# Layer 0's norm: logarithms and exponentials in three batches, centre and squares on VectorE, scaling shared with GpSimd, the last bias part sent from two queues

## What is computed

```python
def _layernorm(x, gamma, beta, eps=1e-05):
    mu = jnp.mean(x, axis=-1, keepdims=True)
    var = jnp.var(x, axis=-1, keepdims=True)
    return (x - mu) * jax.lax.rsqrt(var + eps) * gamma + beta
...
x = _layernorm(pair, gamma, beta)
q = (x @ Wq).reshape(B, L, L, N_HEAD, D_HID) * SCALING
...
bias = x @ Wb
gate = jax.nn.sigmoid(x @ Wg + bg)
attn = jnp.einsum('bijhd,bikhd->bijkh', q, k)
attn = attn + bias[:, None]
attn = jax.nn.softmax(attn, axis=-2)
out = jnp.einsum('bijkh,bikhd->bijhd', attn, v).reshape(B, L, L, N_HEAD * D_HID)
out = gate * out
return out @ Wo + bo
```

## Time and profile before

| | |
|---|---|
| median of 3 runs | 1290.49 us (1289.76 to 1291.64) |
| the profiled execution, device time | 1290.73 us |
| its span, first to last instruction | 1288.9 us |
| PE, PEld, DVE, ACT, POOL busy | 86%, 60%, 56%, 44%, 25% of the span |
| `layer0_norm`'s first matmul | 58.96 us |
| last bias DMA issued | at 155.2 us |
| first L703 of attention | 163.27 us |

### The profile page before, as it was taken

The page is one execution under the profiler, slowest core; times in us unless marked ns, Lnnn a source line. Parts: engine busy times, 40 slices in busy tenths (PEclk is TensorE's granted clock), DMA queues, the critical chain, the costliest instruction groups (busy, mean ns, idle before and its releaser), DMA issues. The chain is left out here.

```text
span 1288.9 us, 25804 instructions
## 1 busy us (share of the span) xinstructions
PE 1104.4 (86%) x9639; PEld 771.7 (60%) x9639; DVE 715.9 (56%) x3496; ACT 569.2 (44%) x1161; POOL 324.7 (25%) x466
## 2 busy tenths in 40 slices
PE   3666288888888886998599999999999999999778
PEld 2422076666666663344477677767776777777577
DVE  2511066666666665222566766676666766676235
ACT  1299466666555553001244444444444444444200
POOL 0100055555555552100012221222122211222211
PEclk9697589999999997998699999999999999999969
DMA  7000000000000000000000000000000000000002
GB/s 151 1 1 4 5 3 2 2 2 2 3 2 2 2 3 1 1 1 9 1 2 1 1 2 2 1 1 2 1 1 2 1 2 1 1 1 1 1 28 108
DMA packets 11488, 11.38 MB, mean 9 GB/s; under 512 B 4324, under 2 KB 9188, under 8 KB 11364
## 3 DMA queue, kind: packets, MB, share of 16 engines
q1 hardware_dynamic: 9266, 9.08, 2.6%
q10 hardware_dynamic: 2098, 0.65, 0.3%
HBM read 5.14 MB, written 4.23 MB: 7 GB/s over the span
## 5 line engine op out<-in xcount | busy, mean ns | idle before, releaser
L1451 PE MATMUL quad<-theta,nat 128*128 128x512 f32 x512 | 240.7, 593 | 0.0
L639 POOL TENSOR_TENSOR nat<-nat,arena 128x512 f32<-128x512 f32 x128 | 132.6, 1048 | 114.6 <-DVE arena L703 114.6
L1258 POOL TENSOR_TENSOR nat<-nat,const 128x512 f32<-128x512 f32 x32 | 40.6, 1268 | 444.0 <-DVE nat L1389 444.0
L1283 ACT ACTIVATE flat<-quad 128x256 f32<-128x256 f32 x256 | 94.9, 384 | 87.5 <-PE quad L1459 72.7
L1459 PEld LDWEIGHTS quad<-flat 128*128 128x128 f32 x768 | 104.6, 190 | 46.5 <-ACT flat L1283 25.1
L1459 PE MATMUL quad<-flat 128*128 128x128 f32 x768 | 123.8, 284 | 2.8 <-ACT flat L1283 1.7
L1451 PEld LDWEIGHTS quad<-theta,nat 128*128 128x128 f32 x512 | 87.5, 191 | 61.7 <-issue 61.7
L703 DVE CUSTOM_DVE_ANT_0 nat<-quad,arena 128x128 f32<-128x128 f32 x512 | 113.2, 282 | 9.8 <-PE quad L788 9.8
L662 ACT ACTIVATE nat<-bank 128x512 f32<-128x512 f32 x128 | 69.6, 595 | 101.7 <-PE bank L796 101.7
L1360 DVE SCALAR_TENSOR_TENSOR flat<-nat,c,duo 128x128 f32<-128x128 f32 x64 | 22.0, 344 | 106.5 <-PE duo L1470 106.5
L667 ACT ACTIVATE nat<-nat 128x512 f32<-128x512 f32 x128 | 77.2, 633 | 5.6 <-POOL nat L639 5.5
(11 more groups left out here) (382 smaller groups left out, 2285.1 us busy)
## 6 DMA issues: line engine op xcount, KB each, us to landing
out<-nat SPq DMA_DIRECT2D x16, 256.0 KB, 2.0
arena<-flat SPq DMA_DIRECT2D x64, 4.0 KB
const<-in_constants ACTq DMA_DIRECT2D x1, 400.5 KB, 3.2
arena<-in_L_conv_Ws SPq DMA_DIRECT2D x1, 240.0 KB
flat<-arena SPq DMA_DIRECT2D x3, 32.0 KB, 4.3
nat<-in_x SPq DMA_DIRECT2D x4, 0.2 KB, 11.9
arena<-in_L_conv_Wq ACTq DMA_DIRECT2D x1, 32.0 KB, 6.1
arena<-in_L_conv_Wk ACTq DMA_DIRECT2D x1, 32.0 KB, 6.7
```

The source lines that it names most:

```text
L639: pool.tensor_tensor(scored, scored, of_head(least[b], h).broadcast_to([128, ROWS, L]), ALU.subtract).then_inc(lowered, 1)
L1258: pool.tensor_tensor(quarters(rem), quarters(rem), ident.unsqueeze(1).broadcast_to([128, ROWS, 128]), ALU.add).then_inc(diag_added, 1)
L1283: act.activation(zs[half][k % 2], m.quad[:, HALF * half:HALF * (half + 1), place * C:(place + 2) * C], ACT.Copy).then_inc(z_ready[half], 1)
L1451: return pe.matmul(m.quad[:, n, :], vT[:, col(n)], m.theta[:, part, :], start=(part == 0), stop=False, skip_group_check=True)
```

## The change

- In `layer0_norm` DVE now reads each PSUM centre once: it adds the shift and writes it to `z` (`keep_centre`, `centre_kept`), and squares it from there into one of four buffers. ACT does neither squares nor bias rows.
- ACT takes logarithms of banks 0 to 7, then their exponentials, then 8 to 11, then 12 to 15. `rstd` of all 16 banks stays in `nat`.
- GpSimd scales banks 0 to 7 (after L463's work), DVE banks 8 to 15 after all its centres; DVE keeps the bias rows.
- PE's variance matmul runs two banks behind the centre. Bias matmuls of chunk 0 come after the variance of bank 9, of chunk 1 after bank 11, of chunks 2 and 3 after bank 15. The shift matmul comes first.
- SP sends chunks 0 to 2 in the block. The 16 DMAs of chunk 3 move into `layer0_attention`'s block: eight on SP at once, eight on ACT after q and k of group 0 are kept.
- `wo` is loaded with the other weights on ACT's queue (ahead of theta_w and alpha_raw) and halved in `load_and_prepare`; `pick` is set there too.

```diff
@@ load_and_prepare
+        (m.wo[:, :], args["L0_conv_Wo"]),
         (theta_raw, args["L2_conv_theta_w"]),
...
+            step(pool.memset(m.pick[:, :, :], 0.0))
+            for h in range(HEADS):
+                step(pool.memset(m.pick[:, h, h:h + 1], 1.0))
...
             dve.tensor_copy(m.c0[:, :], coef[:, 0:1])
+            dve.tensor_scalar(m.wo[:, :], m.wo[:, :], 0.5, None, ALU.mult)
@@ layer0_norm
-    squares = [m.take(CH) for _ in range(2)]
-    logs, rstd = ([m.nat[:, (4 * n + b) * CH:(4 * n + b + 1) * CH] for b in range(4)] for n in range(2))
+    squares = [m.take(CH) for _ in range(4)]
-    LAG = 3
+    LAG = 2
+    BATCH_ENDS = (8, 12, 16)
+    POOL_SCALES = BATCH_ENDS[0]
+    BIAS_AFTER = {LAG + 9: (0,), LAG + 11: (1,), LAG + 15: (2, 3)}
@@ gpsimd
+            for q in range(POOL_SCALES):
+                pool.wait_ge(rstd_ready, q + 1)
+                pool.wait_ge(squared, q + 1)
+                pool.tensor_tensor(m.z[:, cols(q)], m.z[:, cols(q)], rstd(q), ALU.mult).then_inc(z_ready, 1)
@@ scalar
-                    act.activation(squares[q % 2], m.bank[q % 4][:, :], ACT.Square, bias=centre_shift).then_inc(squared, 1)
...
+            done = 0
+            for p in range(BANKS):
+                act.wait_ge(var_made, p + 1)
+                act.activation(rstd(p), m.quad[:, p % 2, :], ACT.Ln, bias=m.eps[:, :]).then_inc(logged, 1)
+                if p + 1 in BATCH_ENDS:
                     act.wait_ge(logged, p + 1)
+                    for n in range(done, p + 1):
+                        act.activation(rstd(n), rstd(n), ACT.Exp, scale=-0.5).then_inc(rstd_ready, 1)
+                    done = p + 1
@@ tensor
+            pe.matmul(m.quad[:, 3, 0:1], away, m.shift2[:, :], start=True, stop=True).then_inc(shift_made, 1)
             pe.wait_ge(m.sem("l1_loaded"), 16 * LOADS1)
...
                     if q >= 4:
-                        pe.wait_ge(z_ready, q - 3)
+                        pe.wait_ge(centre_kept, q - 3)
...
-                if 1 <= q <= BANKS:
-                    p = q - 1
+                if q >= LAG:
+                    p = q - LAG
                     pe.wait_ge(squared, p + 1)
                     if p >= 2:
                         pe.wait_ge(logged, p - 1)
...
-                if q == 1:
+                if q == 4:
                     pe.wait_ge(S("early_spread"), 1)
...
-                    pe.wait_ge(z_ready, 4 * chunk + 4)
+                    if 4 * chunk < POOL_SCALES:
+                        pe.wait_ge(z_ready, 4 * chunk + 4)
+                    else:
+                        pe.wait_ge(late_z_ready, 4 * chunk + 4 - POOL_SCALES)
@@ vector
+            def keep_centre(q):
+                dve.wait_ge(centred, q + 1)
+                dve.tensor_scalar(m.z[:, cols(q)], m.bank[q % 4][:, :], centre_shift, None, ALU.add).then_inc(centre_kept, 1)
+                dve.wait_ge(centre_kept, q + 1)
+                if q >= 4:
+                    dve.wait_ge(var_made, q - 3)
+                dve.tensor_tensor(squares[q % 4], m.z[:, cols(q)], m.z[:, cols(q)], ALU.mult).then_inc(squared, 1)
...
+            def scale(first, end):
...
+                    dve.tensor_tensor(m.z[:, cols(q)], m.z[:, cols(q)], rstd(q), ALU.mult).then_inc(late_z_ready, 1)
...
+                    dve.tensor_scalar(m.bias_rows[:, cols(2 * chunk + r)], m.quad[:, 2 + r, :], m.head_bias[:, :], None,
+                                      ALU.add).then_inc(bias_kept, 1)
...
+            for q in range(10, 14):
+                keep_centre(q)
+            keep_bias(0)
+            keep_centre(14)
+            keep_centre(15)
+            keep_bias(1)
+            scale(POOL_SCALES, 12)
+            keep_bias(2)
+            scale(12, 16)
+            keep_bias(3)
@@ sync
-            for chunk in range(CHUNKS):
+            for chunk in range(CHUNKS - 1):
                 sp.wait_ge(bias_kept, 2 * (chunk + 1))
                 for side in range(2):
...
+                    lay_bias(sp, m, chunk, side)
@@ layer0_attention
-            sp.dma_start(wo, args["L0_conv_Wo"]).then_inc(wo_ready, 16)
+            sp.wait_ge(m.sem("z_bias_kept"), 2 * LAST_CHUNK + 2)
+            lay_bias(sp, m, LAST_CHUNK, 0)
...
             keep_qk(0)
+            act.wait_ge(m.sem("z_bias_kept"), 2 * LAST_CHUNK + 2)
+            lay_bias(act, m, LAST_CHUNK, 1)
...
-            pe.wait_ge(pick_ready, 1)
             project_qk(0)
-            pe.wait_ge(S("wo_halved"), 1)
```

More of the change, by code:

```diff
@@ L511, in _ @@
                         pe.wait_ge(logged, p - 1)
-                    pe.matmul(m.quad[:, p % 2, :], same, squares[p % 2], start=True, stop=True).then_inc(var_made, 1)
-                if q == 1:
+                    pe.matmul(m.quad[:, p % 2, :], same, squares[p % 4], start=True, stop=True).then_inc(var_made, 1)
+                if q == 4:
                     pe.wait_ge(S("early_spread"), 1)
@@ L532, in _, with keep_bias @@
         def _(dve):
+            step = m.chain(dve, "dve")
+            def keep_centre(q):
[6 more added lines that the diff above has]
+            def scale(first, end):
+                for q in range(first, end):
+                    dve.wait_ge(rstd_ready, q + 1)
+                    dve.wait_ge(centre_kept, q + 1)
+                    dve.wait_ge(squared, q + 1)
+                    dve.tensor_tensor(m.z[:, cols(q)], m.z[:, cols(q)], rstd(q), ALU.mult).then_inc(late_z_ready, 1)
+            def keep_bias(chunk):
+                for r in range(2):
+                    dve.wait_ge(bias_made, 2 * chunk + r + 1)
+                    dve.tensor_scalar(m.bias_rows[:, cols(2 * chunk + r)], m.quad[:, 2 + r, :], m.head_bias[:, :], None,
+                                      ALU.add).then_inc(bias_kept, 1)
             dve.tensor_scalar(spread, away, m.scale2[:, :], None, ALU.mult).then_inc(spread_ready, 1)
@@ L536, in _ @@
             dve.wait_ge(shift_ready, 1)
-            step = m.chain(dve, "dve")
+            keep_centre(0)
+            keep_centre(1)
             dve.wait_ge(S("early_turned"), 1)
@@ L542, in _ @@
                               m.turned1[0:C, 256:256 + TAPS].unsqueeze(2).broadcast_to([C, TAPS, C]), ALU.mult).then_inc(S("early_spread"), 1)
+            for q in range(2, 6):
+                keep_centre(q)
             dve.wait_ge(S("early_taps"), 1)
@@ L546, in _, with lay_bias, layer0_attention @@
             dve.tensor_copy(m.taps1[:, 512:TAPS * C], m.quad[0:C + 1, 3, 0:C]).then_inc(S("early_kept"), 1)
[L547 to L550 removed]
+            for q in range(6, 10):
+                keep_centre(q)
+            for q in range(10, 14):
+                keep_centre(q)
+            keep_bias(0)
[6 more added lines that the diff above has]
+            keep_bias(3)
         @block.sync
         def _(sp):
[L554 removed]
+            for chunk in range(CHUNKS - 1):
                 sp.wait_ge(bias_kept, 2 * (chunk + 1))
                 for side in range(2):
[L557 to L565 removed]
+                    lay_bias(sp, m, chunk, side)
+def lay_bias(queue, m, chunk, side):
+    for e in range(2):
+        for h in range(HEADS):
+            row = side * C + 32 * e + h
+            first = 2 * (16 * chunk + 8 * side) + e
+            queue.dma_start(m.bias[first:first + 15:2, h * L:(h + 1) * L],
+                            m.bias_rows[row:row + 1, 2 * chunk * CH:2 * (chunk + 1) * CH]).then_inc(m.sem("bias_laid"), 16)
+def layer0_attention(nc, m):
     ident = m.k("ident", 128)
@@ L580, in layer0_attention @@
     factor, gated = m.take(CH), m.take(CH)
[L581 removed]
+    wo, pick = m.wo, m.pick
     least = [m.take(HEADS * ROWS) for _ in range(2)]
[L583 removed]
     sums = m.take(128)
@@ L628, in _ @@
             step = m.chain(pool, "pool")
-            step(pool.memset(pick, 0.0))
-            for h in range(HEADS):
-                step(pool.memset(pick[:, h, h:h + 1], 1.0))
-            pool.sem_inc(pick_ready, 1)
             for g in range(STEPS0):
```

54 lines of the change are left out of this document (11 added, 43 removed).

## The result

| | before | changed |
|---|---|---|
| median | 1290.12 us (1289.27 to 1291.64, 4 runs) | 1270.15 us (1269.03 to 1271.42, 4 runs) |
| ratio, 95% interval | | 0.9843 (0.983 to 0.9855) |
| span of the profiled run | 1288.9 | 1268.0 (device time 1269.75) |
| DVE's first subtraction | 163.27 | 138.89 |
| from there to the end | 1125.6 | 1129.1 |

The kernel is 20.0 us faster, against 22.4 forecast; 1268.0 was predicted and 1270.15 measured, inside the range. The last two lines of the table show two misses with opposite signs: the first subtraction comes 2.0 us earlier than forecast, and 3.5 us are lost again somewhere behind it.

A forecast was written before the change was run, and what follows sets the result against it. ACT's table loads, logarithms and exponentials (4.5 us a bank), then SP's DMA issues at the block's end, bound it. Summed steps moved DVE's first subtraction from 163.27 to 140.9 (-22.4 us), giving 1268.0 us; range 1262.5 to 1276.

The forecast's parts named there:

- Step 1: Start of layer0_norm: with the shift matmul first, the first centre matmul can start at 60.50 instead of 60.85.
- step 8: Loading wo ahead of two other weights on ACT's queue moves the whole first block later: +0.6 us.
- Steps 2 and 3: Norm: TensorE reaches bank 7's variance at 79.95; after the first logarithms and exponential, GpSimd starts at 82.8.
- Step 4: GpSimd's scalings in the norm: 1.27 us each, four done at 87.9.
- Step 6: Norm: DVE's squares wait while GpSimd's scalings read SBUF; +0.9 us, first bias rows kept at 96.4.
- Step 7: Norm: TensorE's granted clock falls around its idle gap before chunk 0's bias matmuls; +1.2 us, bounds 0 or 2.7.
- Step 9: SP's 48 bias DMA issues at 0.66 us take 31.7, ending at 129.9, without waits between chunks.
- Step 10: Entering attention: block's end 0.7, ACT's eight issues 5.2 after q and k, landing 1.7; first subtraction at 140.9.
- So I add nothing: Groups behind the first subtraction: unchanged instructions, TensorE entering at the lower clock in both kernels, so no term added.
- quicker: Rival in the norm: no fall of the clock and no DVE wait for GpSimd; 1265.9 us, chance 0.20.
- shut DVE out through all eight: Rival in the norm: GpSimd's eight scalings block DVE's square until 93.0; 1269.7 us, chance 0.12.
- low all through the stage: Rival: TensorE's clock stays at the lower level throughout the norm; 1286 us, chance 0.03.

The follow-up runs named there:

- the filler: Changed kernel plus five result-less 512-column matmuls on TensorE ahead of chunk 0's bias matmuls in the norm: 1267.61 us, ratio 0.9823.
- the filler, which gives back 3.9: Changed kernel plus four 512-column matmuls on TensorE at layer 2's start, into a bank nothing reads: 1265.88 us, ratio 0.9815.
- batch of one: Changed kernel with each bank's logarithm followed by its exponential (32 table loads), GpSimd still scaling banks 0 to 7: 1277.0 us, ratio 0.9884.
- one-queue kernel: Changed kernel with all 64 bias DMAs sent by SP alone inside the norm's block: 1277.05 us, ratio 0.9883.
- kernels with half the DMAs: Changed kernel with 32 two-row bias DMAs instead of 64: 1254.12 us; with all scalings on VectorE too: 1252.14 us.

## Why the prediction came out right, and where it was off

- **What bounds the kernel**: right. The stage's end moved with the chain named: first batch, four scalings, chunk 0's bias rows, SP's issues, ACT's issues, landing.
- **Step 1 and step 8, start and load of wo**: 60.50 + 0.6 was forecast for the first centre, and it starts at 60.18. The load shows no effect: DVE's instruction behind ACT starts at 19.12 and 19.46 in the two profiles of before, and between 18.89 and 19.85 in the eleven profiles with the load ahead of it; the first centre matmul starts at 60.85 and 61.00 in the one, at 59.25 to 60.52 in the other. Step 8 was mis-sized: 0 instead of 0.6.
- **Steps 2 and 3, to the first scaling**: 83.4 with step 8's 0.6, measured 82.28. 0.9 of the 1.1 comes from the start.
- **Step 4, the scalings**: 1.29 each against 1.27; with the hand-over to TensorE 5.5 us against 5.1.
- **Step 6, the lock**: DVE's square took 1.23 beside GpSimd, against 0.69 alone, so it exists, as sized (0.5 to 0.9). But DVE then idled 8.39 us for the next centre, so on the path it cost 0 instead of 0.9: TensorE's own wait for the scalings and the lower clock behind it covered the lock. With the clock kept high by the filler it did lie on the path, with 0.9.
- **Step 7, the clock**: it fell and came back, the middle of the bounds. 1.35 on the bias matmuls (3.29 against 1.94) and some 0.4 on the centre behind them, against 1.2 for all. The filler shows what it was worth on the path: 1.1 to 1.5 us until SP's first issue.
- **Step 9, SP**: first rows kept at 97.0 instead of 98.2; 48 issues of 0.67 instead of 0.66, and no pause between chunks. Right.
- **Step 10, into attention**: here the largest error inside the stage. I let ACT issue only after q and k were both kept, but its queue issued the first at 132.01, while L714 ran and ahead of L716. 1.3 us weren't paid. The eight issues took 5.7 instead of 5.2, the landing 1.15 instead of 1.7, the block's end 0.8 instead of 0.7. Together 1.2 less.
- **"So I add nothing"** for the groups behind it: this is the step that failed. The instructions were indeed the same and the reasoning looked at the clock at attention's start alone; the stage where the clock mattered was layer 2's first, 470 us later. Of the 3.5 us lost, 2.5 lie there; the filler, which gives back 3.9, shows that the clock is what they hang on. The 2.0 by which the first subtraction came early hid most of it: that the sum fits the measured time to 2.2 us is in part luck.
- **The rivals**: "quicker" was half right (no lock on the path, but the clock fell). GpSimd didn't shut DVE out through all eight: its square ended after one turn. The clock was neither low all through the stage (it rose at 64.4) nor stayed low behind the gap. ACT's issues cost 0.6 to 0.8, not 4.64. One slip of the sum: 1270.3 for "nothing saved" adds to 1268.3, where the others add to 1268.0.

**The two rules.** In the batch of one, 32 switches still follow each other at 1.28 with 0.01 to 0.02 around them, 3.94 us a bank; with a drain a bank could not be shorter than 0.69 + 0.63 + 2 x 2.66 = 6.6. The figure of 2.66 in the Trainium skill, "ScalarE: Activation LUTs", What ACT_TABLE_LOAD costs, is not what these rows show: the load of 1.28 agrees, the drain doesn't appear.

Issuing: the second queue was worth 2.6 us by the rows of the one-queue kernel (worked out, not run), a little more than the 2.0 of the prediction. That is a saving of issue time, as the Trainium skill, "DMA: Bandwidth & Descriptors", Issuing engines are not separate DMA queues, has it. But its "usually small relative to the DMA itself" doesn't hold for these transfers: the last one landed 1.15 us after its issue had ended, the issues of SP before it took 37 us, and halving their number brought the first subtraction 15.8 us forward.

## What to carry to other kernels

Where many small DMAs leave one queue back to back, count them before speeding up what feeds them: an issue took 0.67 us for 4 KB in one row and 0.54 for 8 KB in two, and a two-row pattern that halves the number gained 16 us, four fifths of what the whole change had gained. Look for the waits inside such a queue too: a merged row of the timeline hides them, and here 20.2 us of them went. A batch was worth here only what its first consumer got earlier, not the engine time it saved. And when an edit shifts all that follows, an untouched stage can still change: compare the distance from the edit to the end, and if it differs, look at the granted clock at the start of every later stage.

## What was not expected of the hardware

- The granted clock rose 2.0 us after layer 2's dense work began in three profiles and 6.5 to 9.1 us after it in seven, all with the same TensorE instructions ahead in that layer; 617.3 and 618.2, or 634.7 and 634.9, for two executions of one kernel. TensorE was busy without a break from 614 to 616 us in the changed kernel, and the clock stood at 0.50. Work whose result nobody reads, put into TensorE's waits, shortened the distance by 3.9 us and the median by 4.3. The Trainium skill, "TensorE: Matmul & The Clock Gate", What's actually happening, says that the number of slow matmuls at a start varies from run to run of one kernel; here it repeated in the two profiles of the two kernels that have two, and varied between kernels; the times of the kernels with half the DMAs hint that it varies within one too.
- The queue of ACT issued DMAs beside its running ACTIVATEs (132.01 and 132.81 beside 132.00 and 132.59).
- An issue of two rows and 8 KB was shorter than one of one row and 4 KB: 0.54 against 0.67 us on SP.
- A DVE square with two SBUF inputs took 1.23 and 1.58 us beside GpSimd's scalings and 0.69 alone. That fits the Trainium skill, "SBUF — State Buffer", SBUF: two separate sides, by which the two engines lock a shared port for a whole instruction.
